# Moving the feed-forward weight quantisation into the cross-attention slots, and the score maximum to the head of VectorE's slot

## The chip, the cores and the metric

The kernel runs on one core of a Trainium2 chip. The metric is the device time of one execution in microseconds (us). A core has five engines that run their own instruction streams and meet only at semaphores: TensorE (PE, matrix products and transposes), VectorE (DVE), ScalarE (ACT), GpSimd (POOL) and SyncE (SP, here only the issuer of DMAs). SBUF is the on-chip memory of 128 partitions; PSUM is the accumulator memory that TensorE writes.

## The reference, cut to what matters

One decoder layer on 64 sequences of 64 tokens and 256 channels, in three parts, each followed by a residual add and a layer norm: self-attention with 16 heads, cross-attention with 16 heads against a context, and a gated feed-forward in which weights and activations are quantised.

```python
def _quant_weight(w):
    scale = jnp.mean(jnp.abs(w)) + EPS
    wq = jnp.clip(jnp.round(w / scale), -1.0, 1.0) * scale
    return w + stop_gradient(wq - w)
def bitlinear(x, w):
    return jnp.einsum('bsi,oi->bso', _quant_act(x), _quant_weight(w))
x = _layernorm(x + attention(x))
x = _layernorm(x + cross_attention(x, ctx))     # softmax(q k^T) v, 16 heads, rope, mask
gate = sigmoid(bitlinear(x, w_gate)); up = bitlinear(x, w_up)     # weights 1024 x 256
x = _layernorm(x + bitlinear(gate * up, w_down))                  # weights 256 x 1024
```

So each of the three feed-forward matrices (262,144 values, held as 128 partitions x 2048) needs the sum of its absolute values over everything, then a scaling with rounding, then a clip to -1, 0, 1. Rounding is done by adding and later subtracting the constant MAGIC (12582912.0).

## The kernel before, in words

The program runs self-attention (to 977 us of the profiled run), a short preparation of cross-attention, the cross-attention itself (998 to 1406 us) and the feed-forward (to 1537 us). Only cross-attention changes.

Cross-attention is a software pipeline written out by hand. The 4096 tokens are 8 tiles of 512; the 16 heads are 8 pairs. A **slot** n stands for tile n // 8 and head pair g = n % 8; there are 64 of them and 19 more (n = 64 to 82) in which the pipeline runs dry. In slot n each engine works on several slots' data at once, given by lags: the queries of slot n, the scores of n-3 (`S_AT`), the normalisation of n-4 (`NORM_AT`), the transposes of n-5 (`T_AT`), the low part of the transposed probabilities of n-6 (`PTL_AT`), probabilities times values of n-7 (`PV_AT`) and the output projection of n-9 (`PROJ_AT`). Products are done in two bf16 parts (high and low), so every f32 operand also needs a low part, which GpSimd (`low_of`, L793) or VectorE makes.

TensorE's order in a slot: scores into `xsP` (L973, L981), `xropeP` (L990) and `xlatP` (L994) of the new queries, the transposes into `xptP` (L1001), probabilities times values into `xoP` (L1014), the projection into `xprojP` (L1026), and then one "other" product of the next or an earlier tile (`other(n)`, chosen by `step(n)`), which also goes to `xoP` and so waits until ScalarE has copied `xoP` to `oA` (semaphore `s_oe`). `xptP` is one buffer: the transposes of a slot wait until VectorE has read those of the slot before (`s_ptl`).

ScalarE's order: eight exponentials (L1069, they need the negated maximum `x_ntop`), `oA` (L1076), `x_pth` (L1089), `qh` (L1094), a copy of the other product, and a layer norm part. VectorE's order: `x_inv` (L1133, reciprocal of the softmax sums), `x_ptl` (L1138), `x_ntop` (L1143, the maximum), `x_turn`, `qh`, `xropeP` (L1152 to L1166), then by g a piece of the next keys (`kf`, L1177) or of the layer norm and the activation scale (`xsc`, L1192). GpSimd's order: `x_probs` times `x_inv` (L1221), the low part of `oB` (L793, its tile is printed as `uqT` since it lies in that buffer), pieces by g (at g = 0 four scalings of `X` into `uqT`, L1233), and last `qhl` (L793). `oB` is `oA` rearranged by four DMAs that SyncE issues; `oB` has two buffers, so the DMAs of slot m wait for the projection of slot m-2.

The three feed-forward matrices are loaded to `okv` at slots 1 to 3. They are used at `WEIGHTS_AT` = 64: in slots 64, 65 and 66 ScalarE sums the absolute values (L1114), after slot 67's projection TensorE adds them over the partitions (L1033), in slots 68 to 70 ScalarE scales and rounds (L1119), and in slots 69 to 71 VectorE clips in two instructions each (L1207, L1209).

Of the kernel before, what the change touches and what calls it, by code (L numbers as in the profile page):

```python
# [603 lines left out]
def cross_weights(a, sem, sb):  # L604
# [17 lines left out]
    def by_rows(name):  # L622
# [9 lines left out]
            "s_weights": s_w, "weights": 9 * 16, "s_seg": s_seg, "s_segf": sem("l_segf"), "s_square": sem("l_square"), "s_ffn": sem("l_ffn"), "s_abs": sem("l_abs"), "w_sums": sb("w_sums", [P, 3], F32)}  # L632
# [183 lines left out]
def cross_attention(nc, a, X, norm, ident, late, ffn, sem, sb, part):  # L816
# [22 lines left out]
    ntop, total, inv = sb("x_ntop", [P, BT], F32), sb("x_total", [P, BT], F32), sb("x_inv", [P, BT], F32)  # L839
# [7 lines left out]
    winv = sb("winv", [P, 3], F32)  # L847
# [12 lines left out]
    s_out, s_kturn, s_kadd, s_kmoved, s_ln1 = (sem("c_" + n) for n in ("out", "kturn", "kadd", "kmoved", "ln1"))  # L860
    s_low_ctx, s_xl, s_qcl, s_kl, s_KVl, s_xs = (sem("c_" + n) for n in ("lowctx", "xl", "qcl", "kl", "KVl", "xs"))
    s_stats, s_mom, s_ln, s_root, s_ln2, s_max, s_sc, s_xinv = (sem("q_" + n) for n in ("stats", "mom", "ln", "root", "ln2", "max", "sc", "xinv"))
    s_sum, s_wsc, s_winv, s_wm, s_wr = (sem("q_" + n) for n in ("sum", "wsc", "winv", "wm", "wr"))
# [5 lines left out]
    WEIGHTS_AT = N  # L869
# [18 lines left out]
    def outs_before(n):  # L888

        return sum(kind not in (None, "kr") for kind in STEPS[:n])  # L890

    def turns_before(n):

        return STEPS[:n].count("kr")

    with nc.Block() as block:
        @block.sync
        def _(sp):
# [12 lines left out]
            for n in range(LAST):  # L911
# [14 lines left out]
                if step(n)[0] == "kr":  # L926
                    wait(sp, s_kturn, turns_before(n + 1))
                    wait(sp, s_kadd, turns_before(n))
                    sp.dma_start(moved_k[0:R, :], turned_k[R:P, :]).then_inc(s_kmoved, 16)
# [7 lines left out]
        def _(pe):  # L937
            def other(n):
# [5 lines left out]
                wait(pe, s_kturn, turns_before(n))  # L944
# [21 lines left out]
            for n in range(LAST):  # L966
# [36 lines left out]
                if has(n, PV_AT):  # L1003
# [5 lines left out]
                    wait(pe, s_kturn, turns_before(n))  # L1009
# [20 lines left out]
                if n == WEIGHTS_AT + 3:  # L1030
                    wait(pe, late["s_abs"], 3)
                    wait(pe, s_lat, N)
                    nc.tensor.matmul(latP[:, 0:3], kept["ones"][:, :], late["w_sums"][:, :], start=True, stop=True).then_inc(s_sum, 1)  # L1033

        @block.scalar
        def _(act):
            def copy_out(n):
                kind, c, tile = step(n)
                if kind in (None, "kr"):
                    return  # L1040
# [82 lines left out]
        def _(dve):  # L1123
# [3 lines left out]
            for n in range(LAST):  # L1127
                j, g = divmod(n, HP)
                if has(n, NORM_AT):
# [3 lines left out]
                    nc.vector.reciprocal(inv[:, :], total[:, :]).then_inc(s_inv, 1)  # L1133
# [34 lines left out]
                if kind == "kr":  # L1168
# [28 lines left out]
                k = n - WEIGHTS_AT  # L1197
                cols = CC * DFF
                if k == 4:
                    wait(dve, s_sum, 1)  # L1200
                    nc.vector.tensor_scalar(wsc[:, :], latP[:, 0:3], 1.0 / (C * DFF), EPS, ALU.mult, ALU.add).then_inc(s_wsc, 1)
                    wait(dve, s_wsc, 1)
                    nc.vector.reciprocal(winv[:, :], wsc[:, :]).then_inc(s_winv, 1)
                if 5 <= k < 8:
                    w = late["okv"][:, (k - 5) * cols:(k - 4) * cols]
                    wait(dve, s_wm, k - 4)
                    nc.vector.tensor_scalar(w, w, MAGIC, 1.0, ALU.subtract, ALU.min).then_inc(s_wr, 1)  # L1207
                    wait(dve, s_wr, k - 4)
                    nc.vector.tensor_scalar(ffn["flat"][k - 5], w, -1.0, None, ALU.max)  # L1209
# [4 lines left out]
        def _(pool):  # L1214
            for n in range(LAST):
                j, g = divmod(n, HP)
                if has(n, NORM_AT):
# [4 lines left out]
                if has(n, PROJ_AT):  # L1222
# [263 lines left out]
```

## Time and profile before

| what | value |
|---|---|
| median of 3 runs | 1541.66 us (1538.03 to 1543.57) |
| the profiled execution, its own time | 1538.94 us |
| its span | 1537.0 us |
| busy, whole span | PE 92%, ACT 82%, POOL 80%, DVE 78% |
| granted TensorE clock, mean | 0.977 |
| slots 0 to 63 | 998.8 to 1351.8 us |
| slots 64 to 82 up to the feed-forward's first product | 1351.8 to 1407.2 us |

The span is the time between the first and the last profiled instruction; the execution's own time has 1.9 us around it. Instructions of an engine overlap a little in the records: the start of one to the start of the next is the engine's pace, and for TensorE a product's end lies later than the start of the next. "Slot 31" below begins with the first score product at 1165.21 us, slot 32 at 1170.48 us.

### The profile page before, as it was taken

How to read it: one execution, taken by the hardware profiler on the slowest of the kernel's cores; microseconds unless marked ns; L12 is line 12 of the kernel's file. 1: busy time of each engine (PE TensorE's matmuls, PEld its weight loads, DVE VectorE, ACT ScalarE, POOL GpSimd, SP SyncE). 2: the span in 40 equal slices, each digit the busy share in tenths (PEclk: the TensorE clock that was granted, in tenths of full speed). 3: DMA queues.
4: the chain of work that ended last, by engine and by line, in shares of the span. 5: the costliest groups of instructions: out<-in, count | busy, mean ns of one | idle time of the engine just before them, and what ended most of it. 6: DMA issues, size and time to landing. Idle time of an engine off the chain costs nothing. (4 is left out here: it accounts for less than half of the span.)

```text
span 1537.0 us, 53907 instructions
## 1 busy us (share of the span) xinstructions
PE 1407.7 (92%) x19782; PEld 1053.3 (69%) x19986; DVE 1196.7 (78%) x2828; ACT 1259.5 (82%) x4038; POOL 1230.3 (80%) x1196
## 2 busy tenths in 40 slices
PE   5998999999999999999999998679999999975997
PEld 3666777777777777777777776446777676763665
DVE  4877787777777777777777778588889888955997
ACT  5876888888888888888888886378999999994776
POOL 5899888888888888888888886358888888852555
PEclk9999999999999999999999999699999999997999
DMA  7700000000000000000000000054334333320011
GB/s 235 181 14 16 3 17 16 3 16 17 4 15 16 6 13 17 10 9 17 14 5 16 3 3 3 4 177 113 109 96 111 108 96 96 96 70 9 15 42 56
DMA packets 58370, 71.66 MB, mean 47 GB/s; under 512 B 14560, under 2 KB 42528, under 8 KB 58112
## 3 DMA queue, kind: packets, MB, share of 16 engines
q1 hardware_dynamic: 58112, 68.22, 15.3%
q8 instruction: 162, 2.65, 0.7%
q14 instruction: 96, 0.79, 0.2%
HBM read 29.39 MB, written 4.19 MB: 22 GB/s over the span
## 5 line engine op out<-in xcount | busy, mean ns | idle before, releaser
L440 DVE SCALAR_TENSOR_TENSOR X<-projP,r,X 128x256 f32<-128x256 f32 x512 | 211.3, 476 | 3.2 <-PE projP L257 3.2
L237 PEld LDWEIGHTS svP<-W,xT 128*128 128x128 bf16 x3072 | 182.3, 98 | 30.3 <-issue 0.2
L503 POOL TENSOR_TENSOR y_sql<-y_sq 128x512 bf16<-128x512 f32 x128 | 133.0, 1039 | 79.5 <-ACT y_sq L324 79.1
L237 PE MATMUL svP<-W,xT 128*128 128x128 bf16 x3072 | 192.4, 219 | 0.0
L208 PE MATMUL qkssP<-xT,W 128*128 128x512 bf16 x641 | 161.8, 383 | 33.3 <-issue 20.2
L208 PE MATMUL kP<-xT,W 128*128 128x512 bf16 x768 | 188.2, 381 | 0.0
L257 PE MATMUL projP<-W,y 128*128 128x256 bf16 x1024 | 178.9, 277 | 3.3 <-POOL yl L503 3.2
L339 ACT ACTIVATE probs<-scores,ntop 128x64 f32<-128x64 f32 x512 | 170.5, 339 | 2.1 <-DVE ntop L430 2.1
L1069 ACT ACTIVATE x_probs<-xsP,x_ntop 128x64 f32<-128x64 f32 x512 | 152.2, 326 | 22.9 <-DVE x_ntop L1143 22.3
L793 POOL TENSOR_TENSOR qhl<-qh 128x1024 bf16<-128x1024 f32 x64 | 121.2, 1893 | 44.4 <-issue 37.5
L503 POOL TENSOR_TENSOR k_sql<-k_sq 128x512 bf16<-128x512 f32 x128 | 133.1, 1040 | 22.0 <-ACT k_sq L344 21.4
L257 PE MATMUL projP<-W,yl 128*128 128x256 bf16 x512 | 141.8, 277 | 0.0
L538 POOL TENSOR_TENSOR ql<-q 128x512 bf16<-128x512 f32 x128 | 139.3, 1088 | 0.0
L208 PEld LDWEIGHTS kP<-xT,W 128*128 128x128 bf16 x768 | 75.6, 98 | 92.3 <-issue 3.0
L503 POOL TENSOR_TENSOR q_sql<-q_sq 128x512 bf16<-128x512 f32 x128 | 133.0, 1039 | 6.6 <-ACT q_sq L331 6.6
L541 POOL TENSOR_TENSOR vl<-v 128x512 bf16<-128x512 f32 x128 | 136.3, 1065 | 0.0
L503 POOL TENSOR_TENSOR yl<-y 128x512 bf16<-128x512 f32 x128 | 133.0, 1039 | 0.0
L470 DVE TENSOR_TENSOR ptl<-pyP,pth 128x256 bf16<-128x256 f32 x128 | 54.3, 424 | 96.8 <-ACT pth L358 96.8
L208 PEld LDWEIGHTS qkssP<-xT,W 128*128 128x128 bf16 x768 | 65.0, 98 | 81.4 <-issue 12.5
L453 DVE COPY v<-svP 128x512 f32<-128x512 f32 x128 | 88.4, 691 | 39.7 <-PE svP L237 38.6
L427 DVE SCALAR_TENSOR_TENSOR scores<-svP,r,bias 128x64 f32<-128x64 f32 x512 | 110.0, 278 | 4.5
L1069 ACT ACTIVATION_READ_ACCUMULATOR x_probs<-xsP,x_ntop 128x1 f32 x512 | 112.2, 219 | 0.0
(252 smaller groups left out, 4914.1 us busy)
## 6 DMA issues: line engine op xcount, KB each, us to landing
x_turned<-x_turn SPq DMA_DIRECT2D x128, 128.0 KB, 2.0
oB<-oA SPq DMA_DIRECT2D x256, 64.0 KB, 2.0
w_stage<-in_wqkvp SPq DMA_DIRECT2D x16, 512.0 KB, 3.2
x_stage<-in_xT SPq DMA_DIRECT2D x8, 512.0 KB, 4.0
X<-in_x SPq DMA_DIRECT2D x1, 4096.0 KB, 16.9
x_stage<-in_ctxT SPq DMA_DIRECT2D x8, 512.0 KB, 4.7
out<-X SPq DMA_DIRECT2D x7, 512.0 KB, 2.9
okv<-in_L_xattn_W_o SPq DMA_DIRECT2D x1, 2048.0 KB, 11.8
```

The lines of the kernel that those rows point to most:

```text
L208: last = nc.tensor.matmul(dst[:, :], weight(parity, u, i, c), xT[:, z, c, tok], start=(c == 0 and k == 0), stop=(c == CC - 1 and k == 2))
L237: last = nc.tensor.matmul(svP[:, b * D:(b + 1) * D], xT[:, u, c, t * TILE + b * P:t * TILE + (b + 1) * P], weight(parity, z, 2, c), start= ...
L257: last = nc.tensor.matmul(projP[:, b * C:(b + 1) * C], y_part, W[:, (j - 3) // NT % 2, z, 3 * CC * D:], start=(i == 0), stop=(i == 2))
L339: last = nc.scalar.activation(probs[:, b, :], scores[:, b, :], ACT.Exp, bias=ntop[:, b:b + 1], accum_out=total[:, b:b + 1])
L427: last = nc.vector.scalar_tensor_tensor(scores[:, b, :], svP[:, b * T:(b + 1) * T], r[:, b:b + 1], row, ALU.mult, ALU.add)
L440: last = nc.vector.scalar_tensor_tensor(acc, projP[:, b * C:(b + 1) * C], r[:, PB + b:PB + b + 1], acc, ALU.mult, ALU.add)
L453: nc.vector.tensor_copy(v[:, j % 4, :], svP[:, :]).then_inc(s_ve, 1)
L503: return nc.gpsimd.tensor_tensor(dst[:, :], src[:, :], high(src, slice(None), 0, TILE), ALU.subtract)
L538: nc.gpsimd.tensor_tensor(ql[:, j % 2, :], q[:, j % 2, :], high_of(q, j % 2), ALU.subtract).then_inc(s_ql, 1)
L541: nc.gpsimd.tensor_tensor(vl[:, j % 4, :], v[:, j % 4, :], high_of(v, j % 4), ALU.subtract).then_inc(s_vl, 1)
L793: return eng.tensor_tensor(dst, src, high_part(src), ALU.subtract)
L1069: last = nc.scalar.activation(probs[:, m % 3, b % PB, b // PB, :], sP[:, b * T:(b + 1) * T], ACT.Exp, bias=ntop[:, b:b + 1], accum_out=tot ...
```

## The change

Three things are changed. The sums of absolute values become six VectorE reductions of 128 x 1024 at the end of its slots 8 to 12 and 16; their sum over the partitions is an "other" product of TensorE in slot 18 (kind `ws`) that goes to `xoP`, and four short VectorE instructions make the scales. Scaling with rounding becomes six GpSimd instructions of 128 x 1024 in slots 22, 30, 38, 46, 54 and 62 (g = 6), before `qhl`. The clip becomes six pairs of VectorE instructions of 128 x 1024 at the end of slots 24, 32, 40, 48, 56 and 64 (g = 0). ScalarE has none of it any more. Second, VectorE takes `x_ntop` first in its slot, ahead of `x_inv` and `x_ptl`; for that the softmax sums get a second buffer. Third, GpSimd takes the low part of `oB` ahead of `x_probs`.

```diff
+    CHUNKS = 2 * 3
+    SUM_AT, SCALE_AT = (8, 9, 10, 11, 12, 16), 18
+    ROUND_AT = tuple(HP * j + 6 for j in range(2, 2 + CHUNKS))
+    CLIP_AT = tuple(HP * (j + 1) for j in range(2, 2 + CHUNKS))
@@ TensorE
+                elif kind == "ws":
+                    wait(pe, late["s_abs"], CHUNKS)
+                    last = nc.tensor.matmul(oP[:, 0:CHUNKS], kept["ones"][:, :], late["w_sums"][:, :], start=True, stop=True)
-                if n == WEIGHTS_AT + 3:
-                    nc.tensor.matmul(latP[:, 0:3], kept["ones"][:, :], late["w_sums"][:, :], ...).then_inc(s_sum, 1)
@@ ScalarE
-                    wait(act, s_inv, m)
+                    wait(act, s_inv, m - 1)
-                if 0 <= k < 3:
-                    nc.scalar.activation(ffn["flat"][k], late["okv"][:, k * cols:(k + 1) * cols], ACT.Abs,
-                                         accum_out=late["w_sums"][:, k:k + 1]).then_inc(late["s_abs"], 1)
-                if 4 <= k < 7:
-                    nc.scalar.activation(w, w, ACT.Identity, bias=ffn["magic"][:, :], scale=winv[:, k - 4:k - 3]).then_inc(s_wm, 1)
@@ VectorE
+                if has(n, S_AT):
+                    wait(dve, s_s, m + 1)
+                    wait(dve, s_exp, m)
+                    nc.vector.tensor_reduce(ntop[:, :], by_token(sP[:, :]), AX, ALU.max, negate=True).then_inc(s_top, 1)
                 if has(n, NORM_AT):
-                    nc.vector.reciprocal(inv[:, :], total[:, :]).then_inc(s_inv, 1)
+                    nc.vector.reciprocal(inv[:, :], total[:, m % 2, :]).then_inc(s_inv, 1)
                 if has(n, PTL_AT):
                     nc.vector.tensor_tensor(ptl[:, m % 2, :], ptP[:, :], pth[:, m % 2, :], ALU.subtract).then_inc(s_ptl, 1)
-                if has(n, S_AT):
-                    nc.vector.tensor_reduce(ntop[:, :], by_token(sP[:, :]), AX, ALU.max, negate=True).then_inc(s_top, 1)
...
+                if n in SUM_AT:
+                    wait(dve, late["s_ffn"], 3 * 16)
+                    nc.vector.tensor_reduce(late["w_sums"][:, k:k + 1], okv[:, chunk(k)], AX, ALU.add, apply_absolute_value=True).then_inc(late["s_abs"], 1)
...
+                if n in CLIP_AT:
+                    wait(dve, s_wm, k + 1)
+                    nc.vector.tensor_scalar(w, w, MAGIC, 1.0, ALU.subtract, ALU.min).then_inc(s_wr, 1)
+                    wait(dve, s_wr, k + 1)
+                    nc.vector.tensor_scalar(out_, w, -1.0, None, ALU.max)
@@ GpSimd
+                if has(n, PROJ_AT):
+                    low_of(nc.gpsimd, oBl[:, m % 2, :], oB[:, m % 2, :]).then_inc(s_ol, 1)
                 if has(n, NORM_AT):
                     nc.gpsimd.tensor_tensor(p_, p_, inv[:, :].unsqueeze(2).to_broadcast([P, BT, T]), ALU.mult).then_inc(s_norm, 1)
-                if has(n, PROJ_AT):
-                    low_of(nc.gpsimd, oBl[:, m % 2, :], oB[:, m % 2, :]).then_inc(s_ol, 1)
...
+                if n in ROUND_AT:
+                    wait(pool, s_winv, 1)
+                    nc.gpsimd.tensor_scalar(w, w, winv[:, k % 3:k % 3 + 1], MAGIC, ALU.mult, ALU.add).then_inc(s_wm, 1)
```

VectorE's program from the end of slot 23 to the start of slot 25, before:

```order
L1196 RECIPROCAL xinv<-xsc 128x4
L1133 RECIPROCAL x_inv<-x_total 128x8
L1138 TENSOR_TENSOR x_ptl<-xptP,x_pth 128x512
L1143 TENSOR_REDUCE x_ntop<-xsP 128x8
L1152 TENSOR_TENSOR x_turn<-xropeP,tabs 128x512
L1161 TENSOR_TENSOR qh<-xropeP,x_turned 64x8x64 x2
L1166 TENSOR_TENSOR xropeP<-xropeP,tabs 128x512
L1133 RECIPROCAL x_inv<-x_total 128x8
```

The same stretch of VectorE's program with the change:

```order
L1195 RECIPROCAL xinv<-xsc 128x4
L1132 TENSOR_REDUCE x_ntop<-xsP 128x8
L1137 RECIPROCAL x_inv<-x_total 128x8
L1142 TENSOR_TENSOR x_ptl<-xptP,x_pth 128x512
L1151 TENSOR_TENSOR x_turn<-xropeP,tabs 128x512
L1160 TENSOR_TENSOR qh<-xropeP,x_turned 64x8x64 x2
L1165 TENSOR_TENSOR xropeP<-xropeP,tabs 128x512
L1214 TENSOR_SCALAR okv<-okv 128x1024
L1216 TENSOR_SCALAR wg<-okv 128x1024
L1132 TENSOR_REDUCE x_ntop<-xsP 128x8
```

The maximum has moved ahead of the reciprocal and of `x_ptl`, and two clips of 128 x 1024 stand between slot 24 and the maximum of slot 25.

GpSimd's program of slot 24 and the head of slot 25 before, where the first L793 of `uqT` is the low part of `oB`:

```order
L1221 TENSOR_TENSOR x_probs<-x_probs,x_inv 128x512
L793 TENSOR_TENSOR uqT<-oB 128x512
L1233 ISA
L1233 TENSOR_SCALAR uqT<-X,xinv 128x256 x4
L793 TENSOR_TENSOR qhl<-qh 128x1024
L1221 TENSOR_TENSOR x_probs<-x_probs,x_inv 128x512
```

And GpSimd's program of slots 22 (which has the first rounding) to 25 with the change:

```order
L793 TENSOR_TENSOR uqT<-oB 128x512
L1233 TENSOR_TENSOR x_probs<-x_probs,x_inv 128x512
L1263 ISA
L1263 TENSOR_SCALAR okv<-okv,winv 128x1024
L793 TENSOR_TENSOR qhl<-qh 128x1024
L793 TENSOR_TENSOR uqT<-oB 128x512
L1233 TENSOR_TENSOR x_probs<-x_probs,x_inv 128x512
L793 TENSOR_TENSOR qcl<-qcf 128x512
L793 TENSOR_TENSOR qhl<-qh 128x1024
L793 TENSOR_TENSOR uqT<-oB 128x512
L1233 TENSOR_TENSOR x_probs<-x_probs,x_inv 128x512
L1240 TENSOR_SCALAR uqT<-X,xinv 128x256 x4
```

The low part of `oB` now stands ahead of `x_probs`, so that what follows a slot's `qhl` directly is an instruction that does not wait for VectorE's slot; the rounding stands ahead of `qhl` in slot 22.

## Rows read from the trace of the kernel before

**Rows 1.** Windows: busy us (count) by engine, granted clock, DMA share, GB/s.

```profile
1165.00:1212.00 47.00, 44.92 (x511) 33.16 (x519) 40.69 (x74) 44.52 (x180) 40.12 (x36) 1.00 0.39 106
```

**Rows 2.** Timeline, TensorE, slots 31 and 32: start, us, instruction, idle before, releaser.

```profile
1165.21 0.19 PE L981 MATMUL xsP<-kf,qh 128*128 128x64 bf16 x1
...
1167.26 0.60 PE L1001 MATMUL xptP<-ident,x_probs 128*128 128x128 f32 x4
...
1168.37 0.38 PE L1026 MATMUL xprojP<-WB,oB 128*128 128x256 bf16 x2
...
1169.57 0.27 PE L1026 MATMUL xprojP<-WB,uqT 128*128 128x256 bf16 x1
1169.86 0.46 PE L963 MATMUL xoP<-ident,kf 64*128 64x64 f32 x4
1170.48 0.19 PE L981 MATMUL xsP<-kf,qh 128*128 128x64 bf16 x1 [0.16 <-issue]
...
1175.64 0.66 PE L952 MATMUL xoP<-ident,X 128*128 128x128 f32 x4 [0.53 <-ACT oA L1076]
```

**Rows 3.** Timeline, ScalarE, slot 31.

```profile
1166.85 0.32 ACT L1069 ACTIVATE x_probs<-xsP,x_ntop 128x64 f32<-128x64 f32 x1
...
1169.17 0.64 ACT L1076 ACTIVATE oA<-xoP 128x512 f32<-128x512 f32 x1
```

**Rows 4.** Timeline, VectorE, slot 31 and its spill into slot 32.

```profile
1165.20 0.20 DVE L1133 RECIPROCAL x_inv<-x_total 128x8 f32<-128x8 f32 x1
1165.32 0.64 DVE L1138 TENSOR_TENSOR x_ptl<-xptP,x_pth 128x512 bf16<-128x512 f32 x1
1166.12 0.69 DVE L1143 TENSOR_REDUCE x_ntop<-xsP 128x8 f32<-128x512 f32 x1 [0.17 <-PE xsP L981]
...
1168.94 0.70 DVE L1166 TENSOR_TENSOR xropeP<-xropeP,tabs 128x512 f32<-128x512 f32 x1
...
1171.13 0.18 DVE L1196 RECIPROCAL xinv<-xsc 128x4 f32<-128x4 f32 x1
...
1171.91 0.68 DVE L1143 TENSOR_REDUCE x_ntop<-xsP 128x8 f32<-128x512 f32 x1
```

**Rows 5.** Timeline, slot 67: transposes that wait for x_ptl.

```profile
1368.81 0.69 DVE L1138 TENSOR_TENSOR x_ptl<-xptP,x_pth 128x512 bf16<-128x512 f32 x1 [0.77 <-ACT x_pth L1089]
...
1369.65 0.69 PE L1001 MATMUL xptP<-ident,x_probs 128*128 128x128 f32 x4 [0.65 <-DVE x_ptl L1138]
```

**Rows 6.** Line L390: durations in ns, minimum, median, maximum.

```profile
L390 DVE TENSOR_SCALAR w_stage<-w_stage,qkw x16: 343/344/1132, 6.9 to 871.5; 128x256 f32<-128x256 f32 x16
```

**Rows 7.** Timelines of GpSimd and VectorE around 117 us.

```profile
116.59 1.17 POOL L538 TENSOR_TENSOR ql<-q 128x512 bf16<-128x512 f32 x1
117.72 1.22 POOL L541 TENSOR_TENSOR vl<-v 128x512 bf16<-128x512 f32 x1
...
116.78 1.27 DVE L395 TENSOR_SCALAR mask<-square 128x512 bf16<-128x512 f32 x1
```

**Rows 8.** Timeline, GpSimd, slot 32 (g = 0).

```profile
1175.32 1.89 POOL L793 TENSOR_TENSOR qhl<-qh 128x1024 bf16<-128x1024 f32 x1
```

**Rows 9.** Groups by line: count, busy us, mean ns, idle before.

```profile
L1207 DVE TENSOR_SCALAR okv<-okv 128x2048 f32<-128x2048 f32 x3 | 3.7, 1217 | 2.4 <-ACT okv L1119 2.4
...
L1192 DVE TENSOR_REDUCE xsc<-X 128x4 f32<-128x1024 f32 x1 | 1.2, 1212 | 0.0
...
L1378 POOL TENSOR_SCALAR hm<-hs,hinv 128x1024 f32<-128x1024 f32 x32 | 35.9, 1120 | 49.1 <-DVE hinv L1412 49.1
```

**Rows 10.** Timeline, slot 66: its first score product, and ScalarE.

```profile
1362.97 0.19 PE L981 MATMUL xsP<-kf,qh 128*128 128x64 bf16 x1
...
1363.45 1.90 ACT L1114 ACTIVATE wu<-okv 128x2048 bf16<-128x2048 f32 x1
```

**Rows 11.** Timeline, GpSimd, low parts of oB in the drain.

```profile
1377.84 1.04 POOL L793 TENSOR_TENSOR uqT<-oB 128x512 bf16<-128x512 f32 x1 [4.64 <-DMA oB<-oA]
...
1387.75 1.88 POOL L793 TENSOR_TENSOR uqT<-oB 128x512 bf16<-128x512 f32 x1 [2.04 <-DMA oB<-oA]
```

More of the change, by code:

```diff
@@ L859, in cross_attention @@
     s_swap, s_ot = [sem("c_swap0"), sem("c_swap1")], [sem("c_ot0"), sem("c_ot1")]
-    s_out, s_kturn, s_kadd, s_kmoved, s_ln1 = (sem("c_" + n) for n in ("out", "kturn", "kadd", "kmoved", "ln1"))
+    s_out, s_read, s_kadd, s_kmoved, s_ln1 = (sem("c_" + n) for n in ("out", "read", "kadd", "kmoved", "ln1"))
     s_low_ctx, s_xl, s_qcl, s_kl, s_KVl, s_xs = (sem("c_" + n) for n in ("lowctx", "xl", "qcl", "kl", "KVl", "xs"))
     s_stats, s_mom, s_ln, s_root, s_ln2, s_max, s_sc, s_xinv = (sem("q_" + n) for n in ("stats", "mom", "ln", "root", "ln2", "max", "sc", "xinv"))
-    s_sum, s_wsc, s_winv, s_wm, s_wr = (sem("q_" + n) for n in ("sum", "wsc", "winv", "wm", "wr"))
+    s_wsc, s_winv, s_wm, s_wr = (sem("q_" + n) for n in ("wsc", "winv", "wm", "wr"))
     s_ctx = late["s_ctx"]
@@ L888, in outs_before, with reads_before, chunk @@
     def outs_before(n):
-        return sum(kind not in (None, "kr") for kind in STEPS[:n])
-    def turns_before(n):
-        return STEPS[:n].count("kr")
+        return sum(kind not in (None, "kr", "ws") for kind in STEPS[:n])
+    def reads_before(n):
+        return STEPS[:n].count("kr") + STEPS[:n].count("ws")
+    def chunk(k):
+        third, half = k % 3, k // 3
+        return slice(third * CC * DFF + half * DFF, third * CC * DFF + (half + 1) * DFF)
     with nc.Block() as block:
@@ L926, in _ @@
                 if step(n)[0] == "kr":
-                    wait(sp, s_kturn, turns_before(n + 1))
-                    wait(sp, s_kadd, turns_before(n))
+                    wait(sp, s_read, reads_before(n + 1))
+                    wait(sp, s_kadd, step(n)[2] - 1)
                     sp.dma_start(moved_k[0:R, :], turned_k[R:P, :]).then_inc(s_kmoved, 16)
@@ L943, in other @@
                 wait(pe, s_out, outs_before(n))
-                wait(pe, s_kturn, turns_before(n))
+                wait(pe, s_read, reads_before(n))
                 if kind == "xq":
@@ L1008, in _ @@
                     wait(pe, s_out, outs_before(n))
-                    wait(pe, s_kturn, turns_before(n))
+                    wait(pe, s_read, reads_before(n))
                     wait(pe, s_KVl, tile)
@@ L1038, in copy_out @@
                 kind, c, tile = step(n)
-                if kind in (None, "kr"):
+                if kind in (None, "kr", "ws"):
                     return
@@ L1171, in _ @@
                     nc.vector.tensor_tensor(by_token(turned_k[:, :]), by_token(oP[:, :]), tabs[:, 2, :].unsqueeze(1).to_broadcast([P, BT, T]),
-                                            ALU.mult).then_inc(s_kturn, 1)
+                                            ALU.mult).then_inc(s_read, 1)
                 if kind == "qc":
                     wait(dve, s_kmoved, 16 * tile)
-                    wait(dve, s_kturn, tile)
+                    wait(dve, s_read, reads_before(n))
                     wait(dve, s_s, HP * (tile - 1))
@@ L1216, in _ @@
                 j, g = divmod(n, HP)
+                if has(n, PROJ_AT):
+                    m = n - PROJ_AT
+                    wait(pool, s_ot[m % 2], 64 * (m // 2 + 1))
+                    wait(pool, s_proj, m - 1)
+                    low_of(nc.gpsimd, oBl[:, m % 2, :], oB[:, m % 2, :]).then_inc(s_ol, 1)
                 if has(n, NORM_AT):
```

49 lines of the change are left out of this document (20 added, 29 removed).

## The prediction

> **What bounds the kernel now.** I read the page first: busy shares of 92, 82, 80 and 78% say only that four engines are nearly full. Then the windows: in a 47 us stretch of the steady slots TensorE is busy 44.9, ScalarE 44.5, VectorE 40.7 and GpSimd 40.1 [rows 1]. So no engine has room to spare, and what matters is the order inside a slot. The timelines of TensorE, ScalarE and VectorE for one slot give that. I count from the first score product of slot 31.
>
> Transposes start at 2.05, the projection at 3.16; its last product starts at 4.36, and at a pace of 0.11 (twelve products from 3.16) TensorE would be free at 4.47. It starts its "other" product at 4.65, and the next slot 0.62 after that, at 5.27 [rows 2]. What it waits for is `oA`: it ends at 4.60 [rows 3]. That goes back over the eight exponentials, which start at 1.64 [rows 3], to the maximum at 0.91, which waited for the scores [rows 4]. So there are two chains per slot, almost equally long: TensorE's own work (4.47) and scores, maximum, exponentials, `oA`, other product (4.65). In slot 32 the maximum comes at 1.43, since VectorE first ends slot 31's scale, 0.83 into slot 32, and then does `x_inv` and `x_ptl` [rows 4]; there the other product starts only at 5.16 [rows 2]. What the change does to either chain decides.
>
> **Maximum first.** The gate of the exponentials no longer has `x_inv` and `x_ptl` ahead of it. But `x_ptl` now comes after the maximum, and the transposes wait for `x_ptl` since `xptP` is one buffer. VectorE cannot fill the time before the scores with `x_ptl` any more. Step by step in slot 31: maximum at 0.91; its pace is about 0.61 (0.69 with the 0.08 by which such records overlap), `x_inv` 0.12 and `x_ptl` 0.64 [rows 4], so `x_ptl` ends at 2.28. Where transposes waited for `x_ptl` they started 0.15 after its end (1369.50 to 1369.65) [rows 5]. So they start at 2.43 instead of 2.05, all behind them moves by 0.38, and TensorE is free at 4.85. The exponentials' chain stays at 4.65 and is no longer the bound: slot 31 grows by 0.20.
>
> Slot 32: VectorE's path from the maximum to the end of `xropeP` was 3.52 (1166.12 to 1169.64) and gets about 0.7 longer, the scale after it takes 1.67 (to 1171.31) [rows 4]. So slot 31's work ends at 0.91 + 4.2 + 1.67 = 6.8, which is 1.3 in slot 32 after a slot of 5.47. The maximum comes at 1.3, the transposes at 2.8, and TensorE is free at 5.24: against 5.16 that is no gain. The other six slots of a tile start their other product between 4.65 and 5.16, so each changes by between +0.20 and about 0. I take +0.55 for a tile, 3.9 for tiles 1 to 7. Bounds: 0 and 0.38 for each of 56 slots (21).
>
> **Sums.** Six reductions of 128x1024, 1.21 each [rows 9]; they read one SBUF tile. VectorE's slot is 0.91 + 4.2 = 5.1 without extras, so in slots 9 and 10, which have no other product and are the shortest, it now runs 0.3 over into the next one. With slot 18's small product and four short VectorE instructions I take +1.0 (0 if VectorE's idle time covers it, 7.3 if all six stand on the path). The first tile and the last, where the exponentials' chain is the longer one, give back about 0.7. This part and the one before: 3.9 + 1.0 - 0.7 = +4.2.
>
> **Rounding on GpSimd.** The same form took 1.12 [rows 9]. In g = 6 slots GpSimd is the engine with most room, and `qhl`, behind the rounding, is needed two slots later. Cost 0, bounds 0 and 6.7 (six on the path).
>
> **Clips.** A clip of 128x2048 took 1.22 [rows 9], so I take 0.61 for 128x1024, 1.22 for a pair. If only that counted, VectorE would end slot 32 about 5.5 + 1.2 = 6.7 after its start, 0.8 into slot 33, just ahead of the scores: free. But GpSimd runs `qhl` at that time, from 4.84 to 6.73 [rows 8]. A VectorE `tensor_scalar` that came while GpSimd was in an instruction took 1132 ns instead of 344 [rows 6]; one at 116.78 took 1.27 and ended 0.29 after GpSimd's instruction of 116.59 had ended (117.76), and the next GpSimd instruction, due then, took 1.22 and ended 0.89 after VectorE's [rows 7]. So each waits for the other's whole instruction, and when both are due they take turns. In slot 32 with the change: the first clip is due at 5.5, starts when `qhl` ends (about 6.8), ends at 7.4. GpSimd's next instruction, the low part of `oB`, is now first in its slot and waits for nothing of VectorE's: it goes at 7.4 and ends at 8.3. Then the second clip, to 8.9. Slot 32 is 5.24 + 0.71 = 5.95 long, so the maximum of slot 33 comes at 2.95 instead of 0.91, and transposes and all behind them with it: +2.05. So for the clips of slots 24, 32, 40, 48 and 56: 5 x 2.05 = +10.2. In slot 64 there is little new work on VectorE, and its pair fits. Bounds for one pair: 0 (not blocked) and 2.4 (GpSimd goes first both times).
>
> The Trainium skill, "SBUF — State Buffer", section "Who interferes with whom", says that a `tensor_scalar` in its two-port mode and a GpSimd instruction never share: the one that issues first holds the port pair to its end, and a `tensor_reduce` never contends. By that rule the sums stay free of GpSimd and the clips do not, and the trace agrees with its 1132 and 1.27. If the two shared the bandwidth instead, a pair would take some 2.4 and end at 7.9, 1.05 past the scores of slot 33, and five pairs would cost 5 us instead of 10. The rule does not say who goes next when both are due.
>
> **The drain.** ScalarE loses three sums of 1.9 and three scalings. In slot 66 the exponentials waited for the second sum, until 1365.35; with slot 31's 1.64 after the first score (1362.97) they would have started at 1364.61: 0.74 [rows 3, 10]. The one of slot 65 I count at 0.2, since its projection stays late. The third, between two copies that the last projections need, I count at 1.5 of at most 1.9 [rows 10]. Low parts of `oB` lie on the chain to the last projection; without the clips the one that took 1.88 takes 1.04 like its neighbour, and one more of the four is of that kind [rows 11]: 2 x 0.84 = 1.7. Sum -4.1, bounds -2.4 and -6.
>
> **Sum.** +4.2 + 10.2 - 4.1 = +10.3. The profiled execution took 1538.94 in all (span 1537.0), so it would be 1549.2; it lies 2.7 below the median of the runs, 1541.66, which would give 1552.0. I take **1551**.
>
> **Rivals.**
> A, the gain that the reordering is open to: 1532.5. If the transposes do not come to wait for `x_ptl`, slot 32's maximum is 0.52 earlier (1.43 to 0.91), two or three slots of a tile gain smaller amounts, 0.8 in a tile, 5 in six and a half tiles, and with the drain's 4.1 and free clips the sum is -9.1. It decides at one point: `x_ptl` must end by 1.90 after the first score (2.05 less 0.15). For it: the exponentials' chain is today's longer one. Against: 0.91 + 0.61 + 0.12 + 0.64 = 2.28.
> B, clips unhindered: 1542. Then 4.2 - 4.1 = +0.1. For it: the first clip is due at 5.5 and `qhl` starts at 4.84, so a GpSimd that is 0.7 later would let the first pass, one 2 us later both. Against: `qhl` waits only for VectorE's `qh`, which ends 0.7 before `xropeP`.
> C, VectorE takes the port twice running: pair ends at 8.0, +1.15 each, 5.8 in all: 1547.
> D, more is on the path: GpSimd, which has no idle time in slots of g = 1 and 2, passes each block on, or the sums and the small product cost 3 more: 1556.
> **Numbers.** The forecast has 0.45, A 0.15, B 0.17, C 0.15, D 0.08. What a measurement can tell from no change is about 0.3%, 4.6 us: 1537.0 to 1546.3. A is faster; B is the same but for 0.02 (0.01 each way); the forecast, C and D are slower. So 0.16, 0.15, 0.69. The range runs from below B to D: 1540 to 1557; the likeliest case's own is 1548 to 1555.
>
> **What would show it.** The transposes (now L1014) wait for `x_ptl` in nearly every slot and start 2.4 after the first score; exponentials still start near 1.64. Clips of about 0.6 when free show as 1.5 or more at g = 0, with a GpSimd instruction in flight, and slots 25, 33, 41, 49 and 57 are some 2 us longer than 26, 34, 42, 50 and 58. From slot 64 to the feed-forward it is 4 us shorter. It would be wrong if clips show 0.6, if `x_ptl` ends before 1.9, or if the drain is unchanged.

## The result and the profile after

The changed kernel takes 1570.99 us (median of 4 runs, 1568.40 to 1573.95); the kernel before, on the same chip, 1539.85 (the three runs above and a fourth). The ratio is 1.0205, 95% interval 1.0188 to 1.0221: slower, 31 us. I forecast slower, 1551, with a range up to 1557. The direction came out, the size is three times too small. In one run of h2 and one of k2 below (2044 and 1792 us) the granted clock was 0.65 and 0.76; they count in those two medians, not in the ratios.

The sharper measure is inside the profile. The 1007 us ahead of the first score product hold no changed instruction, and in the twelve experiments below they took 1000.7 to 1009.7. So I compare two stretches: "slots", from the first score product of slot 3 to that of slot 66, and "drain", from there to the residual sum of the last tile (VectorE's `X<-xprojP,X`). Slots: 356.1 before, 389.2 after, +33.1. Drain: 28.7 and 28.6, where I had forecast -4.1. All that follows the drain is the same (145.3 and 145.1).

Windows of slots 31 to 34 of the changed kernel; the columns are those of [rows 1]:

```profile
1178.07:1183.64 5.57, 5.36 (x64) 3.85 (x63) 5.00 (x9) 5.47 (x23) 4.54 (x4) 1.00 0.29 88
1183.64:1190.12 6.48, 5.31 (x64) 4.05 (x63) 6.30 (x11) 5.19 (x22) 5.46 (x8) 1.00 0.28 83
1190.12:1199.27 9.15, 6.96 (x64) 5.16 (x63) 8.03 (x10) 6.33 (x25) 7.09 (x6) 0.81 0.19 58
1199.27:1204.80 5.53, 5.32 (x65) 4.07 (x64) 4.51 (x9) 4.96 (x21) 4.44 (x5) 1.00 0.31 95
```

Slot 33 is 9.15 long and its granted clock is 0.81; slots 32 and 34 run at 1.00. It was 5.49 before. Slots 25, 41, 49 and 57 look the same (9.13 to 9.43). Together the five are 18.4 longer.

TensorE in slots 31 and 33, answering to [rows 2, 5]:

```profile
1180.49 0.63 PE L1014 MATMUL xptP<-ident,x_probs 128*128 128x128 f32 x4 [0.21 <-DVE x_ptl L1142]
...
1194.53 0.63 PE L1014 MATMUL xptP<-ident,x_probs 128*128 128x128 f32 x4 [2.19 <-DVE x_ptl L1142]
...
1196.60 0.42 PE L1039 MATMUL xprojP<-WB,uqT 128*128 128x256 bf16 x1
1196.82 0.64 PE L1039 MATMUL xprojP<-WB,oB 128*128 128x256 bf16 x2
```

In slot 31 the transposes start at 2.42 (forecast 2.43) and wait for `x_ptl`. In slot 33 they start at 4.41, after 2.19 us without work, and the projection behind them runs at 0.21 us a product where [rows 2] had 0.11.

VectorE in slot 32, and at its end under the clips:

```profile
1183.12 1.22 DVE L1191 TENSOR_REDUCE xsc<-X 128x4 f32<-128x1024 f32 x1
1184.38 1.03 DVE L1193 TENSOR_SCALAR xsc<-xsc 128x4 f32<-128x4 f32 x1
...
1185.54 0.67 DVE L1132 TENSOR_REDUCE x_ntop<-xsP 128x8 f32<-128x512 f32 x1
...
1189.66 2.01 DVE L1214 TENSOR_SCALAR okv<-okv 128x1024 f32<-128x1024 f32 x1
1191.70 1.41 DVE L1216 TENSOR_SCALAR wu<-okv 128x1024 bf16<-128x1024 f32 x1
1193.04 0.68 DVE L1132 TENSOR_REDUCE x_ntop<-xsP 128x8 f32<-128x512 f32 x1
```

GpSimd beside it:

```profile
1184.35 1.04 POOL L793 TENSOR_TENSOR uqT<-oB 128x512 bf16<-128x512 f32 x1
...
1189.23 1.89 POOL L793 TENSOR_TENSOR qhl<-qh 128x1024 bf16<-128x1024 f32 x1
1191.08 1.48 POOL L793 TENSOR_TENSOR uqT<-oB 128x512 bf16<-128x512 f32 x1
```

In slot 31 the exponentials start at 1.64:

```profile
1179.71 0.31 ACT L1078 ACTIVATE x_probs<-xsP,x_ntop 128x64 f32<-128x64 f32 x1
```

The clips go as forecast: the first waits for `qhl`, the low part of `oB` goes next, then the second clip; the maximum of slot 33 comes at 2.92 (forecast 2.95). Not forecast: slot 31's scaling of four numbers (L1193), which spills into slot 32, takes 1.03, as it meets the low part of `oB`, which now follows `qhl` directly.

### The profile page after: what moved, and what is told of

The parts are those of the page before. It is cut to its first block and busy times, and to the rows that moved or that the text cites. A ratio compares the mean times of both kernels' runs of the same rounds, so it can differ in the third digit from the quotient of the medians.

```text
span 1572.1 us, 54122 instructions
## 1 busy us (share of the span) xinstructions
PE 1450.3 (92%) x19986; PEld 1060.3 (67%) x19986; DVE 1218.6 (78%) x2842; ACT 1250.3 (80%) x4029; POOL 1242.4 (79%) x1202
## 5 line engine op out<-in xcount | busy, mean ns | idle before, releaser
L208 PE MATMUL qkssP<-xT,W 128*128 128x512 bf16 x768 | 190.2, 384 | 15.3 <-POOL W L508 12.8
L793 POOL TENSOR_TENSOR qhl<-qh 128x1024 bf16<-128x1024 f32 x64 | 121.2, 1893 | 47.0 <-issue 37.4
L257 PEld LDWEIGHTS projP<-W,y 128*128 128x128 bf16 x1024 | 100.7, 99 | 16.7 <-POOL yl L503 5.2
```

Of the source, the lines that this page charges most:

```text
L208: last = nc.tensor.matmul(dst[:, :], weight(parity, u, i, c), xT[:, z, c, tok], start=(c == 0 and k == 0), stop=(c == CC - 1 and k == 2))
L257: last = nc.tensor.matmul(projP[:, b * C:(b + 1) * C], y_part, W[:, (j - 3) // NT % 2, z, 3 * CC * D:], start=(i == 0), stop=(i == 2))
L793: return eng.tensor_tensor(dst, src, high_part(src), ALU.subtract)
```

## The experiments

Times in us. "Slots" and "drain" are of each profiled run, the median is of all runs of a kernel, and each ratio is to runs of the kernel before that were made beside it (their medians: 1538.96 to 1540.62).

| kernel | median | ratio to before, 95% | slots | drain |
|---|---|---|---|---|
| before | 1539.85 | | 356.1 | 28.7 |
| changed | 1570.99 | 1.0205 [1.0188, 1.0221] | 389.2 | 28.6 |
| h1 old VectorE order | 1554.53 | 1.0105 [1.0075, 1.0135] | 375.0 | 26.9 |
| h2 clips in drain | 1548.97 | 1.0059 [1.0036, 1.0083] | 370.2 | 25.2 |
| h3 old GpSimd order | 1567.80 | 1.0176 [1.0139, 1.0212] | 385.9 | 28.8 |
| h4 TensorE kept at work | 1558.84 | 1.0128 [1.0094, 1.0161] | 381.9 | 26.7 |
| k1 maximum first alone | 1562.85 | 1.0152 [1.0119, 1.0184] | 380.6 | 28.2 |
| k2 old orders, clips in drain | 1538.09 | 0.9987 [0.9971, 1.0002] | 358.6 | 24.9 |
| k3 old orders, clips in slots | 1550.25 | 1.0070 [1.0050, 1.0091] | 368.4 | 29.2 |
| k4 min and max on GpSimd | 1577.76 | 1.0246 [1.0214, 1.0279] | 396.3 | 28.6 |
| m1 k2, other slots for sums and scale | 1538.03 | 1.0000 [0.9982, 1.0018] | 359.0 | 26.1 |
| m2 m1, clips at g = 4 | 1548.27 | 1.0054 [1.0033, 1.0074] | 368.1 | 27.4 |
| n1 k2, scale in slot 20 | 1537.21 | 0.9992 [0.9976, 1.0008] | 358.5 | 25.0 |
| n2 instruction fetch moved | 1567.10 | 1.0192 [1.0166, 1.0218] | 385.8 | 26.5 |

My theory after reading the trace: the clips cost what I forecast, and a half clock adds 1.6 us to each; the rest is small blocks and waits that I had at nothing. The rivals stand with each run.

### h4: is the half clock a cost of its own?

```
-                    for i, (u, z) in enumerate(PASSES):   # latent query products
+                    for i, (u, z) in list(enumerate(PASSES)) * (4 if n - 1 in CLIP_AT else 1):
```

> The changed kernel with the three products of the latent query repeated three more times in the five slots behind the clips (about 2 us of TensorE work of no use, in the stretch in which it waits for x_ptl; the result is the same). Theory: those slots are 1.5 us longer than VectorE's delay explains because TensorE's granted clock falls to half after its 2.2 us wait; with the wait filled the clock stays and each slot goes from 9.15 to about 7.7: 1571 - 7.5 = 1563.5, ratio 1.015. Rival: the clock falls for another reason, or the wait is no cause; then the slots stay at 9.15 or grow by what the added products delay: 1571 to 1573.

Slot 33 is 7.51. The stretch from the transposes to the next slot, the changed kernel first, then this one (columns of [rows 1]):

```profile
1194.53:1199.27 4.74, 4.74 (x33) 3.93 (x34) 3.65 (x5) 3.85 (x17) 4.02 (x4) 0.64 0.15 55
```

```profile
1183.98:1187.07 3.09, 3.04 (x32) 2.83 (x34) 3.01 (x5) 3.09 (x15) 2.41 (x3) 1.00 0.11 40
```

The transposes start at 4.42 (4.41 in the changed kernel), and the same work behind them takes 3.09 instead of 4.74, at a granted clock of 1.00 instead of 0.64. The five slots are 8.0 shorter, and what stays, 10.4 over the kernel before, is the 10.2 that I had forecast for the clips. In all the slots are 7.3 shorter (slots 6 to 8 by 2.0 too, but slots 19 and 64 longer by 2.5) and the drain 1.9; the other 3 us of the median's 12 don't lie in the two stretches.

### h2: the clips moved

```
-    CLIP_AT = tuple(HP * (j + 1) for j in range(2, 2 + CHUNKS))
+    CLIP_AT = tuple(N + 1 + k for k in range(CHUNKS))
```

> The changed kernel with the six clip pairs moved out of slots 24 to 64 into slots 65 to 70, one pair a slot. Theory: the five slots behind the clips (9.15 us each) go back to 5.5 (18.4 us), slot 64 gives 1.5 back, and the drain loses about 1 us because VectorE's clips again hold up GpSimd's low parts: 1571 - 19 = 1552, ratio 1.008. Rival: the half clock in those five slots belongs to their place in the tile and not to the clips, so only the 2.05 us each that the clips occupy VectorE come back: 1561.

The five slots are back at 5.50 to 5.52, so the half clock was theirs and not their place's. The rival falls. Slot 64 stays at 7.62 (5.02 before): its loss is not the clips'.

### h1, h3 and k1: the two orders

```
 h1, in VectorE's slot:  x_inv; x_ptl; maximum        (changed: maximum; x_inv; x_ptl)
 h3, in GpSimd's slot:   x_probs; low part of oB      (changed: low part of oB; x_probs)
 k1:                     the kernel before, with "maximum; x_inv; x_ptl"
```

> The changed kernel, with VectorE's old order in every slot (x_inv, x_ptl, then the score maximum), all else as changed. Theory: of the 31 us lost, the maximum's new place holds about 4 us in the ordinary slots and, through the idle that x_ptl's delay gives TensorE in slots 6 and 7 and the half clock of slot 8, 1.7 us more; in the five slots behind the clips x_ptl comes 0.7 us earlier, so TensorE waits 1.5 instead of 2.2 us there (3.5 us in all). Sum 9 us less than the changed kernel: 1562, ratio 1.015 to the kernel before. Rival: behind the clips the whole chain moves together and the maximum then is what is late, so nothing comes back there, and the maximum's order is worth only 4 us: 1567.

> The changed kernel with GpSimd's old order (x_probs ahead of the low part of oB), all else as changed. Theory: the scaling of 4 numbers at the end of slots 31, 39, 47, 55 and 63 takes 0.17 instead of 1.03 us, which gives back 2.5 us in slots 32 to 56 and 0.9 in slot 64, and the second clip waits for nothing but its own length, so x_ptl comes 0.8 us earlier behind each clip pair (4 us): 1564, ratio 1.016. Rival: x_probs now waits for the delayed x_inv and takes the low part of oB with it, so that in the clip slots the projection is what waits, and only the 3.4 us outside them come back: 1568.

> The kernel before with the first edit alone: VectorE takes the score maximum ahead of x_inv and x_ptl (with the second row of x_total that this needs), GpSimd's order and the weights as before. Theory, from the changed kernel with GpSimd's old order, whose ordinary tiles are 4.4 us longer than before: x_inv is late by the maximum's 0.7 us, x_probs and behind it the low part of oB start later by that, and TensorE's projection waits for them, 0.35 us a slot on top of x_ptl's 0.1 to 0.2. Eight tiles of some 4 us less the stretches where it doesn't bind: about 22 us, 1562, ratio 1.014. Rival (the prediction's sum): only x_ptl counts, 0.55 us a tile, 1544.

h1 gave 16 us, not 9. Slots 26 to 31 and their like are within 0.03 of before, but for slot 50 (0.10 shorter). Behind the clips, where `x_inv` and `x_ptl` follow at once, TensorE waits 0.9 for `x_ptl` and 0.4 and 0.3 further on, and keeps its clock. Window of slot 33 and the two longer waits in it:

```profile
1177.37:1184.68 7.31, 5.63 (x63) 4.02 (x63) 7.20 (x10) 5.58 (x23) 5.25 (x6) 1.00 0.23 68
```

```profile
1180.47 0.63 PE L1014 MATMUL xptP<-ident,x_probs 128*128 128x128 f32 x4 [0.89 <-DVE x_ptl L1137]
...
1182.20 0.38 PE L1039 MATMUL xprojP<-WB,oB 128*128 128x256 bf16 x2 [0.43 <-DVE X L1147]
```

Slots 32, 40 and 48 stay 0.86 too long: that is GpSimd's order.

h3 behaves like neither text: its median, 1567.80, meets the rival's 1568 by luck. Slots 32, 40 and 48 are back at 5.87 and four of the clip slots at 6.55 (slot 57 at 6.99), but nearly every other slot is 0.3 to 0.4 longer than in the changed kernel. k1 came out as its theory said (1562.85 for 1562): in the ordinary slots it has h3's lengths, with no weights work at all, and the slots cost 24.5 us. Its rows show why, slot 31, from 1175.11; VectorE:

```profile
1176.01 0.69 DVE L1133 TENSOR_REDUCE x_ntop<-xsP 128x8 f32<-128x512 f32 x1 [0.80 <-PE xsP L981]
1176.62 0.19 DVE L1138 RECIPROCAL x_inv<-x_total 128x8 f32<-128x8 f32 x1
```

GpSimd and TensorE:

```profile
1176.89 1.05 POOL L1221 TENSOR_TENSOR x_probs<-x_probs,x_inv 128x512 f32<-128x512 f32 x1 [2.23 <-DVE x_inv L1138]
1177.89 1.04 POOL L793 TENSOR_TENSOR uqT<-oB 128x512 bf16<-128x512 f32 x1
```

```profile
1178.99 0.39 PE L1026 MATMUL xprojP<-WB,oB 128*128 128x256 bf16 x2 [0.18 <-POOL uqT L793]
```

`x_inv` is behind the maximum, `x_probs` waits for it, the low part of `oB` stands behind `x_probs`, and the projection waits for that: it starts at 3.88, and the slot is 5.91. So GpSimd's swap is what the maximum's new place needs, and its price is the block of L1193.

### k2, k3 and k4: can the work be had without the orders?

```
 k2 = changed, both old orders, CLIP_AT as in h2
 k3 = changed, both old orders
 k4 = changed, both old orders, and
 k4 (GpSimd):
-    tensor_scalar(w, w, winv, MAGIC, mult, add)
+    tensor_scalar(w, w, winv, 1.0, mult, min); tensor_scalar(w, w, -1.0, MAGIC, max, add)
 k4 (VectorE, between x_turn and qh of slots 28, 36, ... 68):  tensor_scalar(out, w, MAGIC, None, subtract)
 k4 (VectorE): wsc and winv computed in slot 20, not in slot 18
```

> Sums on VectorE in slots 8 to 16 and rounding on GpSimd in six slots as changed, but both engines' old orders and the clips in slots 65 to 70. Theory: neither the sums (0.5 us in slot 11, nothing in the others) nor the rounding costs TensorE anything, slot 19 costs 1 to 2 us through the chain of small operations on the scale, and the drain without ScalarE's six passes is 3.5 us shorter: 1540 + 2 - 3.5 = 1538.5, ratio 0.999. Rival: the drain gives nothing back, as in the changed kernel: 1542.

> The changed kernel's work at the changed kernel's places, with the old orders of both engines. Theory: the scaling of 4 numbers is not blocked (0 in slots 32 to 56), x_ptl stands right behind the clips and ends 0.7 us sooner than in the changed kernel, GpSimd takes x_probs before the low part of oB, so the second clip is free: each clip slot costs 1.0 to 1.3 us, and TensorE's wait is short enough that the granted clock stays. 6 x 1.1 + 2 (slot 19) - 1 (drain): 1548, ratio 1.005. Rival: any clip pair at this place makes TensorE wait long enough for the half clock, 3 us a slot: 1557.

> Both old orders; GpSimd multiplies and takes the minimum, then takes the maximum and adds MAGIC, in two passes one behind the other in slots 22, 30, ... 62 (its idle time there is 2.5 us before the change); VectorE only subtracts MAGIC, one pass of 0.7 us between x_turn and qh of slots 28, 36, ... 68, where GpSimd is idle; the scale's small operations stand in slot 20 instead of 18. The result is the same. Theory: all of it fits in idle time, each tile costs at most 0.3 us, slot 19 nothing, the drain is 3.5 us shorter: 1540 + 1.5 - 3.5 = 1538, ratio 0.9987. Rival: the second pass holds up GpSimd's qhl by 1.1 us in each of six slots, and TensorE waits for it one slot on (6 us more): 1544.

k2 came out as expected, k3 2 us above. In k2 the rounding costs nothing (slots 20 to 55 are within 0.02 of before, but for slot 24's 0.17), and the drain is 3.8 shorter. In k3 the clip slots cost 1.7 each (2.3 in slot 57), more than I thought, and slot 33 keeps a clock of 1.00. k4 missed by 40 us. GpSimd's groups by line (count, busy, mean ns):

```profile
L1261 POOL TENSOR_SCALAR okv<-okv,winv 128x1024 f32<-128x1024 f32 x6 | 22.3, 3714 | 0.1
L1263 POOL TENSOR_SCALAR okv<-okv 128x1024 f32<-128x1024 f32 x6 | 21.8, 3639 | 0.5
```

The same shape with multiply and add took 1120 ns [rows 9]. With a minimum or a maximum it takes 3.3 times that, and slots 23, 31, ... 63 pay 5.7 to 6.5 us each.

### m1, m2 and n1: other places

```
 m1 = k2, SUM_AT = (8, 9, 12, 13, 16, 17), scale as in k4
 m2 = m1, each clip pair between x_turn and qh of slots 28, 36, ... 68
 n1 = k2, scale as in k4
```

> Both engines' old orders, the clips in slots 65 to 70 as in the run with old orders and clips in the drain (1538), and two more moves: the small operations on the scale stand in slot 20 (slot 19 then is as long as before, as the run with GpSimd's clips showed), and the sums of slots 10 and 11 stand in slots 13 and 17, where VectorE has time. Theory: 1.5 us less in slot 19, 0.6 less in slots 10 and 11, the drain 3.8 us shorter than before as long as no instruction fetch falls on oB's DMAs: some 3 us under the kernel before, 1536.5, ratio 0.998. Rival: the sums' new places cost what the old ones did, or the fetch falls on the DMA, which is 1.4 us and a half clock more: 1539, ratio 0.9995.

> As the run before it in this list, but with each pair of clips in slots 28, 36, ... 68, between x_turn and qh, where GpSimd's idle time of 1.6 us lies before and after the change. Theory: the pair is not hindered (0.72 us each), qh comes 1.45 us later and GpSimd's qhl with it; VectorE waits 0.6 us later in that slot anyway, GpSimd catches up half; a tile costs 0.5 to 1 us, and the drain is as short as without them: 1540, ratio 1.000. Rival: qhl holds up x_probs of the next slot and TensorE waits more than 1 us for it, 1.5 us or more a tile: 1546.

> Both engines' old orders, the sums where the change put them, rounding on GpSimd in slots, clips in slots 65 to 70, and the small operations on the scale in slot 20 instead of 18; nothing else. Theory: against the run with old orders and clips in the drain (slots 358.6 us, drain 24.9) slot 19 is 1.6 us shorter and slot 21 0.5 us longer, as in the run before that moved the sums too: 382.4 us from the first score to the residual sum, where the kernel before has 384.8; 2.4 us less, 1537, ratio 0.998. Rival: what slot 19 gives is taken by the slots behind it: ratio 0.9995.

Slot 19 gave its 1.6, but the sums at the end of slots 13 and 17 made slots 14 and 18 1.13 longer: m1's rival. m2 missed (1548 for 1540, the rival had 1546): each pair costs 1.25 in slots 29, 37, 45 and 53 and 2.2 in slot 61, and the drain is 2.3 longer than in n1. n1 is 0.1 better than k2 in the slots: slot 8 took back most of what slot 19 gave (7.19 at a granted clock of 0.64, against 5.98 at 0.79 in k2; the instructions up to there are the same), and slot 21 took 0.45. No version beats the kernel before by what a measurement can tell; k2 (0.9971 to 1.0002) and n1 come nearest.

### n2: where the drain's gain went

```
+                    if g == 0 and tile >= 4:
+                        for _ in range(16):
+                            nc.tensor.matmul(latP[:, 0:8], WQ[:, 0, g, :], qc[0][:, 0:8], start=True, stop=True)
```

> The changed kernel with 64 tiny products (8 columns each, their result overwritten at once by the real product) spread over slots 32, 40, 48 and 56, where TensorE waits over 1 us for VectorE. They move nothing but the place of TensorE's instruction stream at which the next instructions are fetched. Theory: in the changed kernel a fetch of 1.2 us on one DMA engine, 14.5 us behind the last score, falls on oB's DMA, GpSimd's low part starts at 17.2 instead of 15.8, and TensorE, 3.2 us without work, runs the next two projections at half pace. With 64 products more the fetch comes some 6 us earlier, at 8 to 9, between two of oB's DMAs: the low part starts at 15.8, and the drain is 3 us shorter than 28.6 us; 1568. Rival: the late landing is not the fetch's, and the drain stays at 28.6 with the low part at 17.2, wherever the fetch is: 1571.

The drain of the changed kernel, answering to [rows 11], GpSimd then TensorE:

```profile
1415.60 1.04 POOL L793 TENSOR_TENSOR uqT<-oB 128x512 bf16<-128x512 f32 x1 [3.67 <-DMA oB<-oA]
1417.48 1.04 POOL L793 TENSOR_TENSOR uqT<-oB 128x512 bf16<-128x512 f32 x1 [0.83 <-DMA oB<-oA]
1423.16 1.04 POOL L793 TENSOR_TENSOR uqT<-oB 128x512 bf16<-128x512 f32 x1 [4.65 <-DMA oB<-oA]
```

```profile
1416.70 0.41 PE L1039 MATMUL xprojP<-WB,oB 128*128 128x256 bf16 x2 [2.55 <-POOL uqT L793]
...
1419.04 0.63 PE L1039 MATMUL xprojP<-WB,oB 128*128 128x256 bf16 x2
...
1424.26 0.61 PE L1039 MATMUL xprojP<-WB,oB 128*128 128x256 bf16 x2 [3.10 <-POOL uqT L793]
```

No low part takes 1.88 any more, as forecast. But the one of 1415.60 comes 17.2 after slot 66's first score, the projections then run at half pace (0.63 where full pace has 0.38), and the last one waits again. DMA queues between 1412.92 and 1414.42 (packets, MB, share of 16 engines):

```profile
q1 hardware_dynamic: 122, 0.09, 24.6%
q8 instruction: 1, 0.02, 4.9%
```

One instruction packet takes 4.9% of 16 engines in 1.5 us: 1.2 us of one engine, just when `oB`'s data arrive. In n2 that packet comes at 11.0 to 11.5 instead of 14.5 to 15.0. The low part there, timeline of GpSimd (slot 66 starts at 1393.10):

```profile
1406.59 1.04 POOL L793 TENSOR_TENSOR uqT<-oB 128x512 bf16<-128x512 f32 x1 [3.49 <-DMA oB<-oA]
1408.88 1.04 POOL L793 TENSOR_TENSOR uqT<-oB 128x512 bf16<-128x512 f32 x1 [1.25 <-DMA oB<-oA]
```

The one behind the packet's new place starts at 13.5 (12.5 in the changed kernel), the next at 15.8 (17.2). So the delay moves with the packet. I had guessed its place at 8 to 9; it fell on the transfer before, and the drain gained 2.1, not 3. That the median, 1567.10, is near my 1568 is luck: the profiled run's gain of 3.4 in the slots lies in slots 6 to 8, ahead of the first added product. In the other runs, by the packet's own start: in h4 it was at 10.5 and the low part at 13.6. In h2, k2, m1 and n1 it was at 15.3, after the data, and the low part came at 15.8 to 15.9. In h1, h3, k3, k4 and m2 it was at 14.8 to 15.0, and the low part between 16.9 and 17.6. The low part's time goes with the packet in all of these; the drain's length does so only in part. h2, k2 and n1 have the shortest, 24.9 to 25.2, but m1 has 26.1: its granted clock over the drain was 0.91, k2's 1.00.

## Why the prediction was wrong

Step by step, in us of slots and drain:

| step | forecast | measured |
|---|---|---|
| clips, slots 25, 33, 41, 49, 57: VectorE's delay | +10.2 | +10.4 (h4) |
| the same slots: half clock | 0 | +8.0 |
| maximum first, sums, first and last tile | +4.2 | +5.4 |
| slot 8 | in the line above | +1.7 |
| scaling of four numbers, slots 32, 40, 48, 56 | 0 | +2.5 |
| small operations on the weights' scale, slot 19 | in the +1.0 | +2.3 |
| slot 64 | 0 | +2.8 |
| drain | -4.1 | -0.1 |
| sum | +10.3 | +33.0 |

**What held.** Two chains per slot, `x_ptl` ahead of the transposes at 2.4, the exponentials at 1.64, who takes turns with whom under the clips, rounding free of charge (k2). Rivals A, B and C are out by the same rows: `x_ptl` is waited for, both clips are hindered, GpSimd goes between them. Rival D (blocks passed on, small product dearer, 1556) named some of what was missing, but not the clock. Of my own signs of being wrong one came true: the drain is unchanged.

**The failed step: the clips.** "Transposes and all behind them with it: +2.05" took what is behind the transposes at full pace. VectorE's part of this was right. But here a delay of TensorE of 2.05 was 2.19 us without work, and the granted clock fell from 1.00 towards 0.50 (0.64 over the rest of the slot). The trace of before could have warned me. Behind the transposes of [rows 5], in the drain, where TensorE has much idle time, the projection's products come 0.21 apart:

```profile
1371.84 0.42 PE L1026 MATMUL xprojP<-WB,uqT 128*128 128x256 bf16 x1
1372.05 0.64 PE L1026 MATMUL xprojP<-WB,oB 128*128 128x256 bf16 x2
```

h4 puts the price at 1.6 a slot, h2 takes all of it away, and in h1 waits of 0.9, 0.4 and 0.3 in a slot left the clock alone.

What stays open is when the clock falls: the length of the wait alone does not say it. In slot 19 TensorE waits 2.23 for `x_ptl` in the changed kernel and in h2 alike, with the same instructions up to there. In the changed kernel the clock stayed, in h2 it fell. Slot 19 of the changed kernel, then of h2, with the wait and the window of each:

```profile
1104.87 0.63 PE L1014 MATMUL xptP<-ident,x_probs 128*128 128x128 f32 x4 [2.23 <-DVE x_ptl L1142]
1100.43:1109.09 8.66, 6.43 (x67) 4.11 (x65) 7.80 (x20) 5.99 (x24) 7.06 (x6) 1.00 0.32 99
```

```profile
1097.07 1.09 PE L1014 MATMUL xptP<-ident,x_probs 128*128 128x128 f32 x4 [2.23 <-DVE x_ptl L1142]
1092.63:1102.88 10.25, 7.86 (x65) 5.40 (x66) 7.81 (x20) 6.14 (x24) 7.73 (x6) 0.83 0.27 84
```

The difference is 1.6 us again.

**The second: the drain.** I added up waits that vanish: 0.74 + 0.2 + 1.5 + 1.7. They do vanish, and k2 gives 3.8. In the changed kernel an instruction packet delayed one transfer by 1.4 and the clock fell again (0.88 over the drain); both depend on where things land, and the sum of waits says nothing of it. In k3, with the packet at the same place, the gain is gone too.

**Steps at nothing.** Three (slots 32 to 56, slot 19 and slot 64) came from GpSimd's new order and my reading of only the large instructions. The scaling of four numbers (L1194 in the kernel before, L1193 now) had 0.17 because GpSimd's next instruction waited for `x_inv`; with the low part of `oB` first, it does not wait any more. VectorE and GpSimd before, slot 31's end:

```profile
1170.92 0.17 DVE L1194 TENSOR_SCALAR xsc<-xsc 128x4 f32<-128x4 f32 x1
1171.49 1.04 POOL L1221 TENSOR_TENSOR x_probs<-x_probs,x_inv 128x512 f32<-128x512 f32 x1 [0.55 <-DVE x_inv L1133]
```

In slot 18 of the changed kernel VectorE's chain for the scale shows the same:

```profile
1101.54 0.71 DVE L1205 TENSOR_TENSOR wsc<-sums 128x3 f32<-128x3 f32 x1
1102.29 0.97 DVE L1207 TENSOR_SCALAR wsc<-wsc 128x3 f32<-128x3 f32 x1
```

beside GpSimd's

```profile
1100.34 1.89 POOL L793 TENSOR_TENSOR qhl<-qh 128x1024 bf16<-128x1024 f32 x1
1102.19 1.04 POOL L793 TENSOR_TENSOR uqT<-oB 128x512 bf16<-128x512 f32 x1
```

L1205 ends when `qhl` does, L1207 when `uqT` does. The Trainium skill, "SBUF — State Buffer", section "Who interferes with whom", says that a VectorE instruction with two SBUF inputs also meets a GpSimd instruction that reads SBUF; the 0.71 agrees. In slot 20 the two take 0.15 and 0.17, and slot 19 is at 6.33 (n1), 0.1 under before. GpSimd's new order is not all of it: with the old one (k2) L1207 takes 0.17, but L1205, under `qhl`, 0.94, and slot 19 takes 7.91. With the chain in slot 18 it takes 7.5 to 10.2 from run to run; the two runs at 10.2 (h2 and h4) are those in which the clock fell.

In slot 64 both things meet. The transposes start at 3.65 (1.71 before), since `x_ptl` is behind the blocked L1193 and the maximum; that is 1.9 of the 2.8. The other 0.9 are behind them, and the granted clock of the slot is 0.80:

```profile
1388.60 0.63 PE L1014 MATMUL xptP<-ident,x_probs 128*128 128x128 f32 x4 [2.77 <-DVE x_ptl L1142]
```

Slot 8 (1.7) is half pace alone. Over all kernels here it takes 5.40 to 5.43 where its granted clock is 1.00, 5.97 to 6.11 at 0.76 to 0.81, and 7.09 to 7.23 at 0.63 to 0.65; the changed kernel and h2, with the same instructions up to there, took 7.09 and 5.97. What sets it off in one run and not in the next was not tried.

**Maximum first.** In slots 26 to 31 the changed kernel is 0.8 longer, where I had 0.55 for a tile: near enough. But I had called it a cost of the maximum's place alone; k1 shows that alone it costs 24.5, as the projection waits for GpSimd. Both swaps together, without clips in the slots, cost 11.6 (h2 against k2), slots 19, 32 to 56 and 64 included.

## What to carry to other kernels

Where TensorE is 95% busy, price a wait twice: its length, and what runs behind it if the clock falls (1.6 us here behind a wait of 2.2, though not behind every one); the three short waits of h1 were far cheaper than one long one. Where the order of one of two engines that block each other is changed, list every instruction of both, the four-element ones too, and ask what kept them apart until now. An order that two engines share (`x_inv`, `x_probs`, low part, projection) has to be moved as a whole, or left; here leaving it was the cheapest (k2).

## What the runs showed of the hardware

- GpSimd's `tensor_scalar` of 128x1024 f32 took 1.12 us with multiply and add, 3.64 with max and add, 3.71 with multiply and min (k4).
- A VectorE `tensor_scalar` of 128x4 took 0.17 us free and 1.03 when it met GpSimd's instruction of 1.04, and ended with it: the wait had the other's length, not its own.
- TensorE: behind 2.19 us without work, the next 4.74 us had a granted clock of 0.64; the same work behind useless products took 3.09 at 1.00. Behind 2.23 us without work in slot 19 the clock fell in h2 (0.83 over the slot) and stayed at 1.00 in the changed kernel.
- One instruction packet of 0.02 MB took 1.2 us of one DMA engine, and GpSimd's low part, which waits for `oB`'s 64 KB transfers, started 1.0 (n2) to 1.8 us (k3, against k2) later where it met them.
- Code ahead of the first score that is the same in all took 1000.7 to 1009.7 us in the profiled runs: a spread of 9 us, where k2, m1 and n1 differ from the kernel before by less than 3.
